# Attention block with feed-forward on one core: the stores of the maxima rows are issued by ScalarE instead of SyncE

## Chip, core and metric

One core of one Trainium2 chip. The metric is the device time of one execution in microseconds, as the median of several runs. TensorE (PE; PEld is its weight load), VectorE (DVE), ScalarE (ACT), GpSimd (POOL) and SyncE (SP) each run their own list of instructions and meet through semaphores. A DMA is issued by one of the engines and carried out by 16 DMA engines.

## What is computed

The inputs are x (32 batches of 100 tokens, 320 features) and a context (32 batches of 361 tokens, 192 features). There are 20 heads of 16 features, and everything is float32.

```python
h1 = _ln(x, n1_g, n1_b)
x = _attn(h1, h1, q1, k1, v1, o1_w, o1_b, heads) + x
h2 = _ln(x, n2_g, n2_b)
x = _attn(h2, context, q2, k2, v2, o2_w, o2_b, heads) + x
h3 = _ln(x, n3_g, n3_b)
proj = h3 @ ff_w1 + ff_b1
a, g = jnp.split(proj, 2, axis=-1)
ff = a * jax.nn.gelu(g, approximate=False) @ ff_w2 + ff_b2
return ff + x
```

_attn is softmax(q k / 4) v for each head, followed by the output projection.

## The kernel before

Three parts follow one another: a first stage (normalisation and q, k, v of the self attention for all batches, up to about 140 us), the attention loop, and the feed-forward. The change touches the second.

**The maximum rides in the product.** The softmax needs, for each query and head, its largest score. The scores are first formed with queries along the partitions (self_scores, cross_scores), and VectorE takes their negated maxima (maximum). The scores are then formed again with keys along the partitions (scores_for_exp), so that the exponentials can go straight into the product with v. So that the maximum is subtracted there, it is laid into the query operand as additional rows: the stack qs has 128 rows, and rows 0 and 64 hold the maxima's high part and low part against rows of ones in the key stack ks. The way of the maxima is: TensorE transposes them (turn_max, work jobs MT1 for self and MT2 for cross attention), ScalarE copies the high part into max_parts (max_high), VectorE forms the low part (max_low), and two DMAs store the parts into rows 0 and 64 of qs (place_max, which calls store_max). scores_for_exp(a, b, 0, 0), the first of attention a and batch b, waits for their landing on max_landed. Everything up to the DMAs is done in SBUF and PSUM.

**Software pipeline.** A period p handles four batches at once: x = p (exponentials, v products and output of the cross attention), s = p + 1 (its scores and maxima), c = p + 2 (exponentials and output of the self attention, keys and queries of the cross attention) and f = p + 3 (maxima of the self attention). There are 29 periods with a lead_in before and a run_out behind. Within a period each engine has its order of work written out by hand.

- TensorE: scores_for_exp(1, c, g) for the five groups g, between them self_scores(f) and project_kc(c, 0); times_v(1, c, 0 to 4); then scores_for_exp(2, x, g, jt), 15 of them, interleaved with cross_scores(s, 0 to 9), turn_max(1, f), project_kc, project_out(1, c), project_vc and others; turn_max(2, s) is the last. The two banks expin of the products for exponentials are used in turn, so the product number e waits for the exponential e - 2 (probs_made).
- ScalarE: exponential(1, c, 0 to 4), with kc_high(c, 0) behind the third; copy_product(1, c); exponential(2, x, ...), 15 of them, with max_high(1, f), kc_high(c, 1), heads_high(1, c) and kc_high(c, 2) between; then the copies of the period's end.
- VectorE: the maxima, one for each pair of heads of the cross attention, with the low parts, divisions and normalisations between them. cross_scores(s, i + 1) waits for maximum(2, s, i).
- SyncE: all DMA issues, in this order: load_x(f), place_max(1, f), load_context(f), load_qkv1 (load_own, nine DMAs), place_kc(c, 0), place_kc(c, 1), place_q2(c) (seven DMAs), place_max(2, s), store_x2(x), place_kc(c, 2). An issue that waits holds all behind it.

In lead_in SyncE issues place_max for (1, 1), (1, 2) and (2, 0), in run_out for (2, 30) and (2, 31). The function as it stands on SyncE:

```python
def place_max(a, b):
    ...
    sp.wait_ge(*emptied((f"MT{a}", b, 0)))
    if b > 1:
        last = EXP_AT[a, b - 2, G - 1, 0 if a == 1 else 2]
        sp.wait_ge(exp_full[last % 2], last // 2 + 1)
    store_max(sp, qs[a][u], max_parts[a], max_landed[a][u])
```

The first wait is for max_low (it frees the bank of the transpose), the second that the stack's last reader two batches ago is done.

Of the kernel before, what the change touches and what calls it, by code (L numbers as in the profile page):

```python
# [7 lines left out]
F32 = mybir.dt.float32  # L8
# [14 lines left out]
G, HG = 5, 4  # L23
# [81 lines left out]
OWN = 9  # L105


def store_max(sp, stack, parts, landed):
    for part in range(2):
        dst = stack[64 * part:64 * part + 1].rearrange("p a c n -> p (a c) n")  # L110
        sp.dma_start(dst.bitcast(F32), parts[:, part, :].bitcast(F32)).then_inc(landed, 16)


def own_products(pe, banks, queries, keys, i):
# [55 lines left out]
EXP_AT = {job: i for i, job in enumerate(EXP)}  # L170
# [107 lines left out]
def attention_phase(nc, held, early, x_in, ctxT, n1_g, n1_b, qkv1, o1_w, o1_b, n2_g, n2_b, q2_w, k2, v2, o2_w, o2_b,  # L278
# [8 lines left out]
    with ExitStack() as ctx:  # L287
# [19 lines left out]
        qs = {1: [at(f"qs1_{u}", [P, 2, HP, N], own[u]) for u in range(2)], 2: two("qs2_", [P, 2, HC, N], F32R)}  # L307
# [14 lines left out]
        max_landed = {1: sem2("max1_landed"), 2: sem2("max2_landed")}  # L322
# [61 lines left out]
        def emptied(job):  # L384

            k, n = WORK_AT[job]
            return work_empty[k], n + 1
# [10 lines left out]
        def _(sp):  # L398
# [62 lines left out]
            def place_max(a, b):  # L461
                if b is None:
                    return
                u = b % 2
# [5 lines that stand above are left out]
# [67 lines left out]

            def period(x, s, c, f, e):
                load_x(f)
                place_max(1, f)  # L540
                load_context(f)
                load_qkv1(e)
                place_kc(c, 0)
                place_kc(c, 1)
                place_q2(c)
                place_max(2, s)
                store_x2(x)
                place_kc(c, 2)

# [746 lines left out]
        def _(act):  # L1296
# [27 lines left out]
            def kc_high(b, t):  # L1324
                if b is None:
                    return
                job = ("KC", b, t)
                act.wait_ge(*filled(job))
                if b:
                    act.wait_ge(kc_landed[t][(b - 1) % 2], 16 * 3 * ((b - 1) // 2 + 1))  # L1330
                m = 32 * KT[t][1]
                nc.scalar.copy(kc_parts[0:m, 0, t, :], bank(job)[0:m, 0:JP]).then_inc(hi_made["KC"], 1)

            def max_high(a, b):
# [5 lines left out]
                    act.wait_ge(max_landed[a][(b - 1) % 2], 32 * ((b - 1) // 2 + 1))  # L1340
                nc.scalar.copy(max_parts[a][:, 0, :], bank(job)[0:ROWS[a], 0:N]).then_inc(hi_made[f"MT{a}"], 1)

            def copy_vc(b, i):
                if b is None:
                    return
                job, n = ("VC", b, i), JT[i][1]
                act.wait_ge(*filled(job))
                if b == 0 and i == 0:
                    act.wait_ge(ones_set, 1)
                if b > 1:  # L1350
                    act.wait_ge(pv_made, PV_AT[2, b - 2, G - 1] + 1)
                nc.scalar.copy(vc[b % 2][0:n, i, :, 0:DH], heads(bank(job)[0:n, 0:D]))\
                    .then_inc(work_empty[WORK_AT[job][0]], 1)

            def exponential(a, b, g, jt):
                if b is None:
                    return
                e = EXP_AT[a, b, g, jt]
                n = JT[jt][1] if a == 2 else N
                act.wait_ge(exp_full[e % 2], e // 2 + 1)  # L1360
                if e >= NPT:
                    act.wait_ge(pv_made, PV_AT[EXP[e - NPT][:3]] + 1)
                nc.scalar.activation(probs[e % NPT][0:n, :], expin[e % 2][0:n, 0:HG * N], ACT.Exp, scale=SCALE)\  # L1363
                    .then_inc(probs_made, 1)
# [58 lines left out]
            def run_out():  # L1423
                exponential(1, 31, 0, 0)
                exponential(1, 31, 1, 0)
                exponential(1, 31, 2, 0)
                exponential(1, 31, 3, 0)
                exponential(1, 31, 4, 0)
                kc_high(31, 0)
                copy_product(1, 31)  # L1430
                exponential(2, 29, 0, 0)
                exponential(2, 29, 0, 1)
                exponential(2, 29, 0, 2)
                heads_high(1, 31)
                exponential(2, 29, 1, 0)
                exponential(2, 29, 1, 1)
                exponential(2, 29, 1, 2)
                kc_high(31, 1)
                exponential(2, 29, 2, 0)
                exponential(2, 29, 2, 1)  # L1440
                exponential(2, 29, 2, 2)
                exponential(2, 29, 3, 0)
                features_high("T2", 31)
                exponential(2, 29, 3, 1)
                exponential(2, 29, 3, 2)
                copy_q2(31)
                exponential(2, 29, 4, 0)
                q2_high(31)
                exponential(2, 29, 4, 1)
                exponential(2, 29, 4, 2)  # L1450
                copy_product(2, 29)
                copy_vc(31, 0)
                max_high(2, 30)
                kc_high(31, 2)
                exponential(2, 30, 0, 0)
                copy_vc(31, 1)
                exponential(2, 30, 0, 1)
                exponential(2, 30, 0, 2)
                exponential(2, 30, 1, 0)
                exponential(2, 30, 1, 1)  # L1460
                exponential(2, 30, 1, 2)
                copy_vc(31, 2)
                exponential(2, 30, 2, 0)
                exponential(2, 30, 2, 1)
                exponential(2, 30, 2, 2)
                exponential(2, 30, 3, 0)
                heads_high(2, 29)
                exponential(2, 30, 3, 1)
                exponential(2, 30, 3, 2)
                exponential(2, 30, 4, 0)  # L1470
                exponential(2, 30, 4, 1)
                max_high(2, 31)
                exponential(2, 30, 4, 2)
                copy_product(2, 30)
                exponential(2, 31, 0, 0)
                exponential(2, 31, 0, 1)
                exponential(2, 31, 0, 2)
                exponential(2, 31, 1, 0)
                exponential(2, 31, 1, 1)
                exponential(2, 31, 1, 2)  # L1480
                exponential(2, 31, 2, 0)
                exponential(2, 31, 2, 1)
                exponential(2, 31, 2, 2)
                exponential(2, 31, 3, 0)
                exponential(2, 31, 3, 1)
                heads_high(2, 30)
                exponential(2, 31, 3, 2)
                exponential(2, 31, 4, 0)
                exponential(2, 31, 4, 1)
                exponential(2, 31, 4, 2)  # L1490
                tile_high(0)
                tile_high(1)
                copy_product(2, 31)
                heads_high(2, 31)
                tile_high(2)

            def period(x, s, c, f):
                exponential(1, c, 0, 0)
                exponential(1, c, 1, 0)
                exponential(1, c, 2, 0)  # L1500
                kc_high(c, 0)
                exponential(1, c, 3, 0)
                exponential(1, c, 4, 0)
                copy_product(1, c)
                exponential(2, x, 0, 0)
                exponential(2, x, 0, 1)
                max_high(1, f)
                exponential(2, x, 0, 2)
                exponential(2, x, 1, 0)
                exponential(2, x, 1, 1)  # L1510
                exponential(2, x, 1, 2)
                kc_high(c, 1)
                exponential(2, x, 2, 0)
                heads_high(1, c)
                exponential(2, x, 2, 1)
                kc_high(c, 2)
                exponential(2, x, 2, 2)
                exponential(2, x, 3, 0)
                exponential(2, x, 3, 1)
                exponential(2, x, 3, 2)  # L1520
                exponential(2, x, 4, 0)
                exponential(2, x, 4, 1)
                exponential(2, x, 4, 2)
                features_high("T2", c)
                copy_product(2, x)
                copy_vc(c, 0)
                copy_q2(c)
                copy_vc(c, 1)
                q2_high(c)
                heads_high(2, x)  # L1530
                copy_vc(c, 2)
                max_high(2, s)
# [1107 lines left out]
```

## Time and profile before

| | |
|---|---|
| median of 3 runs | 1357.21 us (1355.14 to 1361.05) |
| the profiled execution | 1353.17 us |
| its span, first to last instruction | 1351.3 us |
| granted TensorE clock, mean | 0.991 of full |
| TensorE busy | 1294.8 us |
| VectorE busy | 824.2 us |
| ScalarE busy | 681.8 us |
| GpSimd busy | 381.4 us |
| DMA issues of maxima rows | 128, all by SyncE |

The times of instructions come from the one profiled execution. Busy time counts work, not waiting, and not the issuing of DMAs.

### The profile page before, as it was taken

The numbers are of one execution on the slowest core, as the hardware profiler recorded it, in microseconds if no ns is written. First come the engines' busy times: TensorE is split into PE (matmuls) and PEld (weight loads), VectorE is DVE, ScalarE is ACT, GpSimd is POOL, SyncE is SP. The second block draws the span as 40 slices with busy tenths as digits, with TensorE's granted clock in tenths as the row PEclk, the third lists the DMA queues.
The fourth block names the chain that finished last, engine by engine and source line by source line (L and its number), as shares of the span: only waits on it lengthen the run. The fifth ranks groups of instructions, "written<-read, shape, count | busy, mean of one in ns | idle before, by whom it ended". The sixth has DMA issues, their size and how long they took to land. (4 is left out here: it accounts for less than half of the span.)

```text
span 1351.3 us, 35359 instructions
## 1 busy us (share of the span) xinstructions
PE 1294.8 (96%) x13364; PEld 1202.7 (89%) x13364; DVE 824.2 (61%) x1728; ACT 681.8 (50%) x1558; POOL 381.4 (28%) x545
## 2 busy tenths in 40 slices
PE   5999789999999999999999999999899999999999
PEld 4999678898898899889898898888689999999999
DVE  5555377777777777777777777777664324252521
ACT  4664345565565565565566566565554231313131
POOL 5421212212212212212212212222176243333331
PEclk8999799999999999999999999999999999999999
DMA  4677455445445455445544444443202101010000
GB/s 124 230 256 228 157 152 156 122 131 161 123 127 159 148 146 161 154 141 153 162 127 141 147 127 138 149 128 95 64 24 74 49 2 49 0 49 0 24 1 25
DMA packets 121669, 155.60 MB, mean 115 GB/s; under 512 B 25012, under 2 KB 115372, under 8 KB 121516
## 3 DMA queue, kind: packets, MB, share of 16 engines
q1 hardware_dynamic: 121516, 153.52, 37.3%
q8 instruction: 101, 1.65, 0.5%
q14 instruction: 52, 0.43, 0.1%
HBM read 62.98 MB, written 28.93 MB: 68 GB/s over the span
## 5 line engine op out<-in xcount | busy, mean ns | idle before, releaser
L1363 ACT ACTIVATE probs<-expin 120x400 f32<-120x400 f32 (+2 forms) x640 | 314.4, 505 | 165.5 <-PE expin L702 108.2
L1037 DVE TENSOR_REDUCE neg_max<-score 100x2 f32<-100x722 f32 x320 | 290.1, 907 | 62.1 <-PE score L676 49.4
L702 PE MATMUL expin<-qs,ks 128*120 128x200 f32 (+2 forms) x1280 | 236.1, 275 | 14.2 <-DMA qs<-max_parts 7.9
L702 PEld LDWEIGHTS expin<-qs,ks 128*120 128x120 f32 (+2 forms) x1280 | 191.9, 179 | 33.3 <-DMA qs<-max_parts 17.5
L676 PE MATMUL score<-ks,qs 128*100 128x362 f32 x640 | 165.5, 340 | 5.6 <-DVE neg_max L1037 4.2
L2427 DVE SCALAR_TENSOR_TENSOR hidden<-ps_a,b_cols,gelu 128x320 f32<-128x320 f32 x100 | 55.1, 551 | 165.1 <-PE ps_a L2351 165.1
L1550 POOL TENSOR_TENSOR var_eps<-mv,eps 100x1 f32<-100x1 f32 x32 | 6.1, 190 | 419.5 <-DVE mv L1105 419.5
L2589 POOL TENSOR_TENSOR hid_lo<-hidden,hid_hi 128x320 fp32r<-128x320 f32 x100 | 87.9, 879 | 122.4 <-ACT hid_hi L2497 122.2
L2509 ACT ACTIVATE gelu<-ps_g,b_cols 128x320 f32<-128x320 f32 x100 | 52.7, 527 | 136.9 <-PE ps_g L2351 136.9
L125 DVE TENSOR_REDUCE neg_max<-score 100x10 f32<-100x1000 f32 x62 | 74.4, 1200 | 54.2 <-PE score L118 54.2
L1570 POOL TENSOR_TENSOR ctx_hi<-ctx_raw,one 128x724 fp32r<-128x724 f32 x32 | 44.6, 1393 | 192.0 <-issue 177.6
L676 PEld LDWEIGHTS score<-ks,qs 128*100 128x100 f32 x640 | 83.0, 166 | 17.1 <-DVE neg_max L1037 6.5
L725 PE MATMUL attn<-probs,vc 120*17 120x100 f32 (+1 forms) x3840 | 96.5, 250 | 0.1
L2351 PE MATMUL ps_g<-t_hi,w_hi 128*128 128x320 f32 x300 | 92.2, 312 | 1.8 <-DVEq L2266 1.8
L725 PEld LDWEIGHTS attn<-probs,vc 120*17 120x17 f32 (+1 forms) x3840 | 80.2, 97 | 13.0 <-issue 7.8
L2351 PE MATMUL ps_a<-t_hi,w_lo 128*128 128x320 f32 x300 | 91.6, 311 | 0.0
L2351 PE MATMUL ps_a<-t_hi,w_hi 128*128 128x320 f32 x300 | 91.6, 310 | 0.0
L2351 PE MATMUL ps_g<-t_hi,w_lo 128*128 128x320 f32 x300 | 91.4, 310 | 0.0
L2368 PE MATMUL ps_y<-w_hi,hid_hi 128*128 128x320 f32 x250 | 78.5, 314 | 0.0
L2369 PE MATMUL ps_y<-w_lo,hid_hi 128*128 128x320 f32 x250 | 77.2, 309 | 0.0
L2370 PE MATMUL ps_y<-w_hi,hid_lo 128*128 128x320 f32 x250 | 77.1, 309 | 0.0
L1810 PE MATMUL qk_ps<-ks,w_qkv 128*128 128x400 f32 x320 | 68.8, 359 | 2.9 <-issue 2.9
(201 smaller groups left out, 2960.9 us busy)
## 6 DMA issues: line engine op xcount, KB each, us to landing
ks<-kc_parts SPq DMA_DIRECT2D x192, 181.0 KB, 3.0
qk_dram<-qk_parts SPq DMA_DIRECT2D x32, 500.0 KB, 5.2
qs<-q_parts SPq DMA_DIRECT2D x192, 75.0 KB
ks<-qk_dram SPq DMA_DIRECT2D x96, 125.0 KB
ctx_raw<-in_ctxT SPq DMA_DIRECT2D x64, 180.5 KB
ks<-kc_parts SPq DMA_DIRECT2D x96, 90.5 KB, 2.2
qs<-qk_dram SPq DMA_DIRECT2D x64, 125.0 KB
v_dram<-v_rows SPq DMA_DIRECT2D x32, 132.8 KB
```

The costliest lines, as they stand in the source:

```text
L125: return nc.vector.tensor_reduce(neg_max[:, :, n * i:n * (i + 1)], src, AX_X, ALU.max, negate=True)
L676: mm = pe.matmul(score[0:N, a, 0:JP], qs[2][u][:, a, q_slot(c), :], ks[2][u][:, c, :], start=True, stop=True)
L702: mm = pe.matmul(dst, ks[a][u][:, c, j0:j0 + n], qs[a][u][:, :, q_slot(c) if a == 2 else c, :], start=True, stop=True)
L725: mm = pe.matmul(attn[32 * i:32 * i + D1, g * N:(g + 1) * N], v, probs[EXP_AT[a, b, g, jt] % NPT][0:n, i * N:(i + 1) * N], start=(jt == 0) ...
L1037: ins = nc.vector.tensor_reduce(dst, src, AX_X, ALU.max, negate=True)
L1363: nc.scalar.activation(probs[e % NPT][0:n, :], expin[e % 2][0:n, 0:HG * N], ACT.Exp, scale=SCALE)\
L1810: mm = pe.matmul(qk_ps[m % 4][:, 0:W], w, a, start=(i == 0), stop=(i == 7))
L2351: mm = pe.matmul(bank[:, 0:W], a, b, start=(k == 0), stop=(k == len(passes) - 1))
L2368: pe.matmul(y, hid_hi[:, f, c], w2_hi[:, f, :], start=(f == 0), stop=False)
L2369: pe.matmul(y, hid_hi[:, f, c], w2_lo[:, f, :], start=False, stop=False)
L2370: mm = pe.matmul(y, hid_lo[:, f, c], w2_hi[:, f, :], start=False, stop=(f == FT - 1))
L2589: nc.gpsimd.tensor_tensor(hid_lo[:, f, c], hidden[n % 2][:], hid_hi[:, f, c].bitcast(F32), ALU.subtract).then_inc(hid_lo_made, 1)
```

## The change

Of the places in a period, place_max(1, f) and place_max(2, s) are taken out of SyncE's list. ScalarE gets a place_max of its own: for the cross attention of batch x in front of the third exponential of the next period (the batch that was s is then x), for the self attention of batch f behind exponential(2, x, 1, 2). Batch 29's is issued in run_out, and batch 0's stays in SyncE's lead_in, as do the others of lead_in and run_out. The semaphores and the data are the same.

```diff
-def store_max(sp, stack, parts, landed):
+def store_max(queue, stack, parts, landed):
     for part in range(2):
         dst = stack[64 * part:64 * part + 1].rearrange("p a c n -> p (a c) n")
-        sp.dma_start(dst.bitcast(F32), parts[:, part, :].bitcast(F32)).then_inc(landed, 16)
+        queue.dma_start(dst.bitcast(F32), parts[:, part, :].bitcast(F32)).then_inc(landed, 16)
...
             def period(x, s, c, f, e):
                 load_x(f)
-                place_max(1, f)
                 load_context(f)
                 load_qkv1(e)
                 place_kc(c, 0)
                 place_kc(c, 1)
                 place_q2(c)
-                place_max(2, s)
                 store_x2(x)
                 place_kc(c, 2)
...
+            def place_max(a, b):
+                act.wait_ge(*emptied((f"MT{a}", b, 0)))
+                if b > 1:
+                    last = EXP_AT[a, b - 2, G - 1, 0 if a == 1 else 2]
+                    act.wait_ge(exp_full[last % 2], last // 2 + 1)
+                store_max(act, qs[a][b % 2], max_parts[a], max_landed[a][b % 2])
+
...
             def run_out():
                 exponential(1, 31, 0, 0)
                 exponential(1, 31, 1, 0)
+                place_max(2, 29)
                 exponential(1, 31, 2, 0)
...
             def period(x, s, c, f):
                 exponential(1, c, 0, 0)
                 exponential(1, c, 1, 0)
+                if x:
+                    place_max(2, x)
                 exponential(1, c, 2, 0)
...
                 exponential(2, x, 1, 1)
                 exponential(2, x, 1, 2)
+                place_max(1, f)
                 kc_high(c, 1)
                 exponential(2, x, 2, 0)
```

## Rows read from the trace of the kernel before

**Rows 1.** The page's first part: busy time, share of the span, instructions.

```profile
PE 1294.8 (96%) x13364; PEld 1202.7 (89%) x13364; DVE 824.2 (61%) x1728; ACT 681.8 (50%) x1558; POOL 381.4 (28%) x545
```

**Rows 2.** 29 periods: busy PE, PEld, DVE, ACT, POOL; clock, DMA share, GB/s.

```profile
187.50:929.20 741.70, 728.39 (x9280) 663.50 (x9281) 554.84 (x1044) 448.92 (x1044) 163.58 (x174) 1.00 0.47 141
```

**Rows 3.** Who waited for whom, 190 to 950 us: total, times, longest.

```profile
PE expin L702 <- DMA qs<-max_parts: 7.9, 16, 1.1
...
PEld expin L702 <- ACT probs L1363: 1.1, 4, 0.6
```

**Rows 4.** Transposes of the maxima, all 29 periods, then one period alone.

```profile
L687 PE MATMUL work<-identf,neg_max x59: 245/247/253, 187.6 to 929.2; 100*24 100x100 f32 x30, 100*20 100x100 f32 x29
...
L687 PE MATMUL work<-identf,neg_max x3: 247/247/251, 776.1 to 801.3; 100*24 100x100 f32 x2, 100*20 100x100 f32 x1
```

**Rows 5.** Timeline of SyncE's issues: start, duration, line.

```profile
569.34 3.74 SPq L457 DMA_DIRECT2D qs<-q_parts  x6
573.19 1.66 SPq L111 DMA_DIRECT2D qs<-max_parts  x2
574.89 0.49 SPq L475 DMA_DIRECT2D x_dram<-x  x1
...
579.87 1.59 SPq L111 DMA_DIRECT2D qs<-max_parts  x2
```

**Rows 6.** Timeline of the other engines at the cross maxima, same period.

```profile
571.72 0.23 ACT L1341 CAST max_parts<-work 24x100 fp32r<-24x100 f32 x1 [1.34 <-PE work L687]
...
571.99 0.25 DVE L1056 TENSOR_TENSOR max_parts<-work,max_parts 24x100 fp32r<-24x100 f32 x1 [0.69 <-ACT max_parts L1341]
...
573.08 0.90 ACT L1363 ACTIVATE probs<-expin 100x400 f32<-100x400 f32 x2 [0.57 <-PE expin L702]
...
575.64 1.05 PE L725 MATMUL attn<-probs,vs 100*17 100x100 f32 x40
...
577.42 0.46 PE L702 MATMUL expin<-qs,ks 128*120 128x200 f32 x2 [0.72 <-DMA qs<-max_parts]
```

**Rows 7.** Timelines: store and use in a waiting period, then in one without.

```profile
266.99 1.65 SPq L111 DMA_DIRECT2D qs<-max_parts  x2
...
270.01 0.46 PE L702 MATMUL expin<-qs,ks 128*120 128x200 f32 x2 [0.49 <-DMA qs<-max_parts]
...
803.08 1.66 SPq L111 DMA_DIRECT2D qs<-max_parts  x2
...
806.55 0.46 PE L702 MATMUL expin<-qs,ks 128*120 128x200 f32 x2
```

**Rows 8.** SyncE's issues that write qs, whole span: duration min/median/max in ns.

```profile
L457 SPq DMA_DIRECT2D qs<-q_parts x192: 538/594/1802, 164.9 to 951.6; - x192
L111 SPq DMA_DIRECT2D qs<-max_parts x128: 727/787/1583, 136.7 to 971.3; - x128
```

**Rows 9.** ScalarE's queue: semaphore instructions before the third exponential and kc_high.

```profile
L1362 ACTq EVENT_SEMAPHORE  x1: 17/17/17, 573.1 to 573.1; - x1
...
L1330 ACTq EVENT_SEMAPHORE  x1: 17/17/17, 573.3 to 573.3; - x1
```

**Rows 10.** Timeline behind exponential (2, x, 1, 2), same period.

```profile
581.20 0.51 ACT L1363 ACTIVATE probs<-expin 121x400 f32<-121x400 f32 x1 [0.56 <-PE expin L702]
...
581.60 0.46 ACT L1332 CAST kc_parts<-work 128x362 fp32r<-128x362 f32 x1
...
581.94 0.53 ACT L1363 ACTIVATE probs<-expin 120x400 f32<-120x400 f32 x1
...
582.33 0.43 ACT L1302 CAST t_hi_OT<-work 128x300 fp32r<-128x300 f32 x1
...
583.24 0.70 PEld L593 LDWEIGHTS work<-w_o,t_hi_OT 128*100 128x100 f32 x5
...
583.33 0.91 DVE L1037 TENSOR_REDUCE neg_max<-score 100x2 f32<-100x722 f32 x1
...
584.60 0.26 PEld L676 LDWEIGHTS score<-ks,qs 128*100 128x100 f32 x2
```

## Prediction

> **What bounds the kernel now.** I read the page's head first: TensorE is busy for 96% of the span, ScalarE for 50% [rows 1]. That is an average over three parts; the change touches only the middle one, the 29 periods of the attention loop, so I cut that stretch out. From 187.5 to 929.2 us TensorE is busy 728.39 of 741.70 us at full clock, ScalarE 448.92 [rows 2]. So TensorE's own order of work sets the time, and a wait counts only where TensorE stands still. The table of waits names those places: the first products of a pair wait for the landing of the maxima rows (7.9 us on the matmuls), while its weight loads wait for ScalarE's exponentials 1.1 us [rows 3]. I then asked how long a period is. The transposes of the maxima stand once per half period, 59 of them from 187.6 to 929.2 us, so 29 periods take 741.6 us, 25.57 each [rows 4]. The period from 776.1 to 801.3 has no such wait and takes 25.23 us [rows 4]. The difference, 0.34 us, times 29 is 9.9 us: all that a better landing of the maxima can give, 0.7%.
>
> Where it comes from: SyncE issues the six stores of q2 back to back (3.74 us), and only then begins the two maxima stores at 573.19, though VectorE had finished the rows at 572.24 [rows 5, 6]. TensorE wants them at 577.42 and has stood 0.72 us [rows 6]. From issue to that use it takes 3.02 us in a usual waiting period (266.99 to 270.01) [rows 7]; in a period where the stores begin at 803.08 the use at 806.55 has no wait [rows 7]. There are slower ones, as at 573.19 (4.2 us). The maxima for the self attention (stored at 579.87, used a period half later) are waited for by nobody.
>
> **The change part by part.** Two stores in each of 58 places (29 for each attention) go from SyncE's queue to ScalarE's: 116 of 128 DMA issues; 12 stay. Nothing is added on another engine, and the data is the same.
>
> *What an issue costs.* No DMA is issued by ScalarE in this trace. The nearest rows are the same stores on SyncE: 727 ns at least, 787 median [rows 8], a pair 1.59 or 1.66 us [rows 5]. The cheapest store of any kind here is 0.49 us, the q2 stores 594 ns [rows 5, 8]. I take D = 1.6 us for a pair, with 1.0 (two at 0.49) and 2.8 (two at 0.8, each also waiting for one of SyncE's at 0.59) as ends. I take it that ScalarE runs nothing that stands behind an issue until it is over. When may it begin? The semaphore instructions between ScalarE's operations tell: the one in front of the third exponential runs at 573.1, when the wait of the second (started 573.08) has just been met, and the one in front of the copy of kc runs at 573.3, before the third exponential has started [rows 9]. So ScalarE's queue runs ahead of execution, but not past an instruction that still waits. The stores begin when the exponential before them starts.
>
> *Place A, cross maxima, after the second self exponential.* Start 573.1, as early as SyncE at its best (1.77 us after the transpose of the maxima at 801.31, here 1.66) and never held by the q2 stores. 3.02 us later is 576.1, TensorE needs them at 576.7 once its times-V products are over. Thus the 0.34 us go. In exchange the third exponential waits for the issues: 573.15 + D, then steps of 0.39 and 0.34 us (to a copy of kc and from it, as at 581.94 and 581.60 [rows 10]), 0.40 us to the fifth exponential and its 0.50 us (a pair takes 0.90 [rows 6]) end at 574.8 + D = 576.4. The last times-V group, of five in 1.05 us from 575.64, begins at 576.48 [rows 6]. So D = 1.6 just fits, about 0.05 us too much; every tenth more of D is a tenth more of period. Place A: -0.29 us.
>
> *Place B, self maxima, after exponential (2, x, 1, 2).* It starts at 581.20, and the copy of kc at 581.60, an exponential at 581.94 and the copy of the turned heads at 582.33, ending 582.76, follow without a gap [rows 10]. With the issues the first starts at 581.25 + 1.59 + 0.05 = 582.89, 1.29 us late, and the turned heads are ready at 584.05. TensorE loads its weights for project_out at 583.24, 0.48 us after the heads before; now, with 0.05 us for the signal (an estimate: the copy that ends at 571.95 frees VectorE at 571.99 [rows 6]), it stalls 0.86 us (the products into the expin bank that the delayed exponential frees stall 0.7 of it). VectorE's low part of the heads comes behind that copy, then its maximum of 0.91 us, on which the next cross_scores waits: 584.12 + 0.47 + 0.91 = 585.50 against TensorE's 584.60 + 0.86 = 585.46 [rows 10]; about 0.1 us more. Place B: +0.95 us, or D - 0.65. Nothing later absorbs it: the free period has hardly an idle TensorE, and all chains of the second half start from project_out.
>
> *What SyncE gains.* store_x2 and the last kc stores begin up to 1.7 us earlier, and load_context and the nine loads of load_own are no longer behind the wait of place_max(1, f). The loop's table of waits [rows 3] has no entry of TensorE for their tiles, so 0. Were they late, the next self_scores would pay. But they now run while ScalarE issues, in both places: SyncE's stores and own loads follow one another there for microseconds, as its six q2 stores do [rows 5].
>
> The Trainium skill, page "DMA: Bandwidth & Descriptors", section "Issuing engines are not separate DMA queues", says that issuing from several engines saves only the time of the sequencer, usually small beside the transfer. By the rows it is 1.66 us of 3.02, over half [rows 5, 7]; were it small, place B would cost nothing and the change would give its 9.9 us or less.
>
> *Sum.* 29 x (-0.29 + 0.95) = 29 x 0.66 = 19.1 us. The profiled execution took 1353.17 us (span 1351.3), 4 us under the median of 1357.21; 1372.3 on its scale is 1376.3 on that of the median. The break-even is at D = 0.99: (D - 0.65) - 0.34 = 0.
>
> **The rivals.**
> *R1, one descriptor generator.* If ScalarE's issue must wait while SyncE's is being served, each store takes up to 0.59 us more [rows 8]. D = 2.8: place B 2.15, place A -0.34 + 1.2 = 0.86, together 3.0 us, 87 us, 1444 us. If only half of an issue excludes the other, D = 2.2: 1.55 + 0.26 = 1.8 us, 52 us, 1410 us. For it: both engines issue at once in A and B. Against: no row shows it, all packets are SyncE's. The Trainium skill has this rule: "Perfetto Trace Analysis", section "DMA Instruction — HWDGE (DVE, Sync)", has a lock on the descriptor generator, shared by two sequencers. No run here shows it yet.
> *R2, the other side: ScalarE issues cheaply.* At D of 0.65 or less place B costs nothing and the whole 9.9 us come in: 1347 us; at D = 0.99 no change. For it: 0.49 us for the x2 store. Against: the same stores have no case under 0.727 us in 128.
> *R3, the landing isn't earlier.* The change does not do what it is for: the small stores, now beside SyncE's kc stores instead of behind q2, still land late, as at 573.19. Then A gives nothing: 29 x (0.95 + 0.05) = 29 us, 1386 us. For it: waits of over 0.7 us occur also where SyncE began at its earliest. Against: 3.02 us repeats.
>
> **How the numbers follow.** Forecast, D between 1.5 and 1.75 a pair: chance 0.48, 1376 us, its own range 1369 to 1386. R3 0.08. R1 0.21, half of it above 1410. R2 0.16 for a gain over 0.5% (6.8 us, what a measurement of this kernel can tell from no change), and 0.07 for between. So faster 0.16, same 0.07, slower 0.77. The range goes from 1347, R2's full gain, to 1412, R1's half price; some 0.12 lies outside.
>
> **What the profile after would show.** 116 issues on ScalarE of about 0.8 us each (R1: 1.1 or more, R2: under 0.5). The third exponential of a period 1.6 us behind the second. The wait for the landing gone from TensorE's table, and new ones there, for the exponential's expin bank and for the turned heads, together about 0.9 us a period, near place B. Periods of 26.2 us with TensorE's clock unchanged. Wrong I would be if ScalarE went on with arithmetic during an issue, if the issue began before the exponential in front had its input, or if TensorE found the lost 0.9 us again in the second half.

## The result and the profile after

The changed kernel takes 1384.68 us (median of 6 runs, 1381.05 to 1386.62) against 1356.18 us for the kernel before in the same rounds: a ratio of 1.0199, 95% interval 1.0178 to 1.0220. It is slower by 28.5 us; the forecast was 19.1 us slower, at 1376. The profiled execution has a span of 1382.8 us, 31.5 more than before.

The page's first part after the change, to be held against [rows 1]: the same instructions, TensorE 22 us busier, and a span that grew more. Of the 22 us, 14.7 lie in the loop. Part of them is the way in which a product behind a stall is recorded, with 0.46 us instead of 0.36 at place B; the rest wasn't followed up. The second fence is the page's part on DMA queues; queue 10 is new.

```profile
PE 1316.7 (95%) x13364; PEld 1207.6 (87%) x13364; DVE 828.8 (60%) x1728; ACT 677.6 (49%) x1558; POOL 382.0 (28%) x545
...
q10 hardware_dynamic: 3828, 1.03, 0.3%
```

The length of the loop comes first, as in [rows 4], from the row of the same transposes after the change.

```profile
L685 PE MATMUL work<-identf,neg_max x59: 246/247/253, 188.8 to 957.1; 100*24 100x100 f32 x30, 100*20 100x100 f32 x29
```

29 periods take 768.3 us instead of 741.6: 26.7 us of the 31.5 lie in the loop. What TensorE waits for there is in the table of waits after, 190 to 965 us; it answers to [rows 3].

```profile
ACT kc_parts L1330 <- issue: 33.2, 28, 1.7
DVE kc_parts L1054 <- ACT kc_parts L1330: 30.8, 30, 3.2
...
PEld expin L700 <- ACT probs L1368: 25.2, 32, 1.4
...
PE expin L700 <- ACT probs L1368: 15.2, 29, 1.1
...
PE expin L700 <- DMA qs<-max_parts: 4.7, 6, 1.2
```

The wait for the landing went from 16 times and 7.9 us to 6 times and 4.7 us. In its place stands a wait of TensorE for an exponential, 29 times in 29 periods. The first line shows whose doing it is: ScalarE stands 1.2 us before its copy of kc, in 28 periods, with no input missing ("issue").

The stores themselves, from the rows of the tile qs, against [rows 8]:

```profile
L111 ACTq DMA_DIRECT2D qs<-max_parts x116: 724/742/1332, 197.7 to 958.7; - x116
...
L111 SPq DMA_DIRECT2D qs<-max_parts x12: 751/803/1279, 136.1 to 1000.7; - x12
```

An issue by ScalarE takes 742 ns in the median, 45 ns less than one by SyncE before, and as long at its shortest.

**Place B, self maxima.** Timelines of ScalarE, VectorE and TensorE after the change in one period; the operations are those of [rows 10], 12.08 us earlier on the clock.

```profile
569.12 0.50 ACT L1368 ACTIVATE probs<-expin 121x400 f32<-121x400 f32 x1 [0.55 <-PE expin L700]
569.18 1.50 ACTq L111 DMA_DIRECT2D qs<-max_parts  x2
570.78 0.46 ACT L1330 CAST kc_parts<-work 128x362 fp32r<-128x362 f32 x1 [1.16 <-issue]
571.13 0.51 ACT L1368 ACTIVATE probs<-expin 120x400 f32<-120x400 f32 x1
571.53 0.42 ACT L1300 CAST t_hi_OT<-work 128x300 fp32r<-128x300 f32 x1
...
571.98 0.47 DVE L1049 TENSOR_TENSOR t_lo_OT<-work,t_hi_OT 128x300 fp32r<-128x300 f32 x1 [0.17 <-ACT t_hi_OT L1300]
572.37 0.90 DVE L1035 TENSOR_REDUCE neg_max<-score 100x2 f32<-100x722 f32 x1
...
571.69 0.29 PEld L700 LDWEIGHTS expin<-qs,ks 128*121 128x121 f32 x2 [0.80 <-ACT probs L1368]
571.70 0.46 PE L700 MATMUL expin<-qs,ks 128*121 128x200 f32 x2 [0.48 <-ACT probs L1368]
572.09 0.95 PE L591 MATMUL work<-w_o,t_hi_OT 128*100 128x320 f32 x5
```

The issues begin 0.06 us after the start of the exponential in front of them, last 1.50 us, and the copy of kc follows 0.10 us behind their end: 1.66 us after the exponential instead of 0.40, so 1.26 us late (forecast 1.29). The product into the bank that the delayed exponential frees stalls, its weight load by 0.80 us, and project_out runs behind it, 2.97 us after the exponential's start. Before it was 583.33 - 581.20 = 2.13, from this row of TensorE:

```profile
583.33 0.90 PE L593 MATMUL work<-w_o,t_hi_OT 128*100 128x320 f32 x5
```

That is 0.84 us lost. The turned heads were ready at 571.95, and TensorE has no wait for them in the table: by the profile the wait that ended last was the one for the bank.

**Place A, cross maxima.** The same for the third self exponential, against [rows 6].

```profile
561.66 0.50 ACT L1368 ACTIVATE probs<-expin 100x400 f32<-100x400 f32 x1 [0.57 <-PE expin L700]
561.72 1.51 ACTq L111 DMA_DIRECT2D qs<-max_parts  x2
563.33 0.50 ACT L1368 ACTIVATE probs<-expin 100x400 f32<-100x400 f32 x1 [1.17 <-PE expin L700]
...
564.07 0.91 ACT L1368 ACTIVATE probs<-expin 100x400 f32<-100x400 f32 x2
...
564.27 1.13 PE L723 MATMUL attn<-probs,vs 100*17 100x100 f32 x40
565.33 0.46 PE L700 MATMUL expin<-qs,ks 128*120 128x200 f32 x2
```

Here the stores land in time: 3.61 us from their beginning to the use, which has no wait. The times-V products are stretched, 1.13 us for 1.05, as the last group meets the delayed fifth exponential: that one ends at 564.98 and the group begins at 565.04. (The row calls the third exponential's wait "PE expin", but those products were done by 561.81; what it waited for was the issue.) In another period the landing is late although it began as early, at 428.37:

```profile
432.99 0.46 PE L700 MATMUL expin<-qs,ks 128*120 128x200 f32 x2 [0.93 <-DMA qs<-max_parts]
```

### The profile page after: what moved, and what is told of

Read it like the earlier page. It is cut to its first block and busy times, and to the rows that moved or that the text cites. A ratio compares the mean times of both kernels' runs of the same rounds, so it can differ in the third digit from the quotient of the medians.

```text
span 1382.8 us, 35359 instructions
## 1 busy us (share of the span) xinstructions
PE 1316.7 (95%) x13364; PEld 1207.6 (87%) x13364; DVE 828.8 (60%) x1728; ACT 677.6 (49%) x1558; POOL 382.0 (28%) x545
## 5 line engine op out<-in xcount | busy, mean ns | idle before, releaser
L700 PE MATMUL expin<-qs,ks 128*120 128x200 f32 (+2 forms) x1280 | 241.1, 279 | 26.5 <-ACT probs L1368 16.4
```

Of the source, the lines that this page charges most:

```text
L700: mm = pe.matmul(dst, ks[a][u][:, c, j0:j0 + n], qs[a][u][:, :, q_slot(c) if a == 2 else c, :], start=True, stop=True)
```

## Experiments

The period splits at the two transposes of maxima. The first half (cross transpose to self transpose, mostly 6.3 to 7.5 us) holds place A, the second (19 us) place B. The two columns of halves are means over the 29 periods, from the starts of the transposes in the timeline; "landing" is TensorE's matmul row for the landing of maxima in the table of waits, 190 to 950 us (965 for the change). Each ratio is to the kernel before in the same rounds. Its median there was 1356.18 beside the change, 1356.36 beside cross_only, self_only, self_late and self_half, 1354.30 beside sync_early and cross_earlier, and 1356.80 beside clear_early.

| kernel | median us | ratio to before (95%) | first half | second half | landing |
|---|---|---|---|---|---|
| before | 1356.18 | | 6.68 | 18.89 | 7.9 |
| the change | 1384.68 | 1.0199 (1.0178 to 1.0220) | 6.69 | 19.80 | 4.7 |
| cross_only | 1355.45 | 0.9985 (0.9966 to 1.0005) | 6.75 | 18.94 | 6.5 |
| self_only | 1383.17 | 1.0198 (1.0162 to 1.0233) | 6.62 | 19.81 | 6.2 |
| self_late | 1353.98 | 0.9981 (0.9959 to 1.0003) | 6.64 | 18.88 | 3.7 |
| self_half | 1358.44 | 1.0019 (1.0000 to 1.0039) | 6.65 | 19.07 | 7.6 |
| sync_early | 1362.74 | 1.0063 (1.0042 to 1.0084) | 6.86 | 18.95 | 2.7 |
| cross_earlier | 1357.36 | 1.0020 (1.0004 to 1.0037) | 6.71 | 18.88 | 2.6 |
| clear_early | 1347.61 | 0.9933 (0.9914 to 0.9952) | 6.38 | 18.90 | 0.2 |

**cross_only and self_only: one place each.** cross_only puts the self attention's stores back on SyncE, self_only the cross attention's.

```diff
 # cross_only, from the changed kernel
                 load_x(f)
+                place_max(1, f)                # SyncE
                 load_context(f)
...
                 exponential(2, x, 1, 2)
-                place_max(1, f)                # ScalarE
```

```diff
 # self_only, from the changed kernel
                 place_q2(c)
+                place_max(2, s)                # SyncE
                 store_x2(x)
...
                 exponential(1, c, 1, 0)
-                if x:
-                    place_max(2, x)            # ScalarE, and the one in run_out
```

> Only the cross attention's stores are issued by ScalarE; the self attention's stay with SyncE. Theory 1 (the cost is the delay of the ScalarE operations behind the stores at the self attention's place; at the cross attention's place the saved landing wait and a new delay cancel): the half period from the cross transpose to the self transpose keeps its mean of about 6.7 us, the other half is back at 18.88, the time is 1356 to 1359. Theory 2 (every issue by ScalarE costs the same, wherever it stands): half of the 28.5 us, 1370.

> Only the self attention's stores are issued by ScalarE. Theory 1: half periods of 19.77 instead of 18.88 us, 29 x 0.9 = 26 us, so 1382. Theory 2: 1370.

The whole loss is in self_only (27 us, second half 19.81); cross_only can't be told from before. Both have 58 issues by ScalarE, so the cost isn't one of issuing as such. TensorE's wait for an exponential follows the place too. This is its row in the table of waits, first of self_only, then of cross_only:

```profile
PE expin L701 <- ACT probs L1369: 15.2, 29, 1.1
...
PE expin L701 <- ACT probs L1369: 0.7, 2, 0.4
```

**self_late: the same 116 issues, one place moved.**

```diff
                 exponential(2, x, 1, 2)
-                place_max(1, f)
                 kc_high(c, 1)
...
                 exponential(2, x, 3, 1)
+                place_max(1, f)
                 exponential(2, x, 3, 2)
```

> All 116 stores stay with ScalarE, but the self attention's are moved seven exponentials later, in front of exponential (2, x, 3, 2), where ScalarE stood idle for 1.75 us waiting for TensorE. Theory 1: the issues lie in that gap, the second half period is back at 18.9 us, the time is 1356 to 1360. Theory 2 (each issue costs), or theory 3 (SyncE's loads, now earlier, are what costs): nothing changes, 1385.

The loss is gone, 1353.98 us. ScalarE's timeline shows the two issues in a gap that was there anyway (the exponential behind waits 1.75 us for TensorE's attn products, as long as before). SyncE's loads come early here too: load_context begins 0.6 us before the self transpose in the median period, in the change 1.0 us before it, in the kernel before 2.9 us behind it. So the earlier loads aren't the cause either.

```profile
585.57 1.04 ACT L1368 ACTIVATE probs<-expin 120x400 f32<-120x400 f32 x2 [0.65 <-PE expin L700]
586.16 1.52 ACTq L111 DMA_DIRECT2D qs<-max_parts  x2
588.36 0.90 ACT L1368 ACTIVATE probs<-expin 121x400 f32<-121x400 f32 x2 [1.75 <-PE attn L723]
```

**self_half: half the issue time at place B.** From self_only; ScalarE stores the high row, SyncE the low row at its old place.

```diff
                 exponential(2, x, 1, 2)
-                place_max(1, f)
+                place_max(1, f, which=(0,))    # ScalarE: high parts
                 kc_high(c, 1)
...
                 load_x(f)
+                place_max(1, f, which=(1,))    # SyncE: low parts
                 load_context(f)
```

> At the self attention's place ScalarE issues only the store of the high parts (0.75 us); SyncE issues that of the low parts and both cross stores, as before. Theory 1, a margin of about 0.45 us before TensorE stands: the copy of kc starts 0.5 us late, TensorE stands at most 0.1 us a period, 0 to 3 us in all, so 1356 to 1360. Theory 2, proportional to the issues: half of 26, 1369.

ScalarE's timeline, one period:

```profile
586.05 0.51 ACT L1370 ACTIVATE probs<-expin 121x400 f32<-121x400 f32 x1 [0.56 <-PE expin L702]
586.11 0.73 ACTq L111 DMA_DIRECT2D qs<-max_parts  x1
586.94 0.46 ACT L1332 CAST kc_parts<-work 128x362 fp32r<-128x362 f32 x1 [0.38 <-issue]
```

The copy of kc comes 0.89 us after the exponential instead of 0.40, and half the issue time leaves a seventh to a fifth of the cost: the second half is 19.07 us (median 19.01 against 18.88), the time 1358.44, 0.19% over before, which is just clear of no change. The loss isn't proportional to the issues. There is a margin: 0.49 us of delay cost 0.13 to 0.18 us, 1.26 us cost 0.91, so it is 0.3 to 0.4 us (expected was 0.45).

**sync_early: the landing without ScalarE.** All stores on SyncE, the cross maxima's in front of the last two q2 stores.

```diff
                 for slot, part in ((0, 0), (2, 0), (1, 1)):
                     if part:
+                        place_max(2, s)
                         sp.wait_ge(*emptied(("QT", b, 0)))
```

> All stores stay with SyncE as in the kernel before, but the two cross stores are issued in front of the last two of the six q2 stores, so they begin as soon as VectorE has made the rows (about 0.85 us after the transpose instead of 1.75 to 2.97). Theory 1 (the landing wait is SyncE's queue, and a landing delayed by an instruction fetch needs about 1.2 us more): the wait for the landing goes, first half periods of 6.35 throughout, 29 x 0.33 = 9.6 us less, 1347. Rival (the landing is late through other transfers, whenever it is begun): no change, 1356.

This missed: 0.63% slower. The maxima do go out early, 0.8 to 1.4 us after the transpose in all but the first period, and the landing waits fall to 2.7 us, 2.3 of them in that first period. But the two q2 stores behind them are late now. They are used directly after the maxima: cross_scores of the next batch waits for q2_landed one product later. The timelines of SyncE and TensorE:

```profile
578.01 1.66 SPq L111 DMA_DIRECT2D qs<-max_parts  x2
579.72 1.24 SPq L458 DMA_DIRECT2D qs<-q_parts  x2
...
582.40 0.46 PE L702 MATMUL expin<-qs,ks 128*120 128x200 f32 x2
583.54 0.55 PE L676 MATMUL score<-ks,qs 128*100 128x362 f32 x2 [0.68 <-issue]
```

The profile names no releaser for the 0.68 us ("issue"); that it is q2_landed is read from the code. In the table of waits, 190 to 950 us, the line stands 12 times with 7.7 us, once behind the loop with 1.5. My expectation had looked at who waits for the maxima and not at who waits for what they were put in front of.

**cross_earlier: place A one exponential earlier.** From self_late.

```diff
                 exponential(1, c, 0, 0)
-                exponential(1, c, 1, 0)
                 if x:
                     place_max(2, x)
+                exponential(1, c, 1, 0)
                 exponential(1, c, 2, 0)
```

> All 116 stores by ScalarE, the self ones late as in self_late, the cross ones one exponential earlier, in front of the second self exponential. Theory 1: they begin at 0.85 instead of 1.70 us after the transpose and land in time in every period, also beside an instruction fetch; but the second exponential starts at 2.45 instead of 1.64, and the product that uses its bank again stalls 0.35 us. First half periods 6.7 us, all alike, 1354 to 1358. Rival: landings are as late as before in some periods, and the stall comes on top, 1365.

The landing waits go, but for 2.6 us, 2.5 of them in the first period. The first half has a floor (its usual shortest value) of 6.56 us instead of self_late's 6.46: the stall at the exponentials eats what the landing gives. 1357.36 us against 1354.30, no gain.

**clear_early: the queue shortened where it was idle.** All stores on SyncE in the old order; clear_max, which writes rows 0 and 64 and needs no q2, goes in front of the wait for q2.

```diff
             def place_q2(b):
...
-                sp.wait_ge(hi_made["Q2"], b + 1)
                 cross_stack_free(b, G - 1)
                 clear_max(sp, qs[2][u], zeros, q2_landed[u])
+                sp.wait_ge(hi_made["Q2"], b + 1)
```

> Everything stays with SyncE; only the clearing store of a period's q2 (clear_max) is issued in front of the wait for the q2 rows, in which SyncE stood idle, instead of behind it. So the six q2 stores and the two cross stores all begin 0.6 us earlier; the cross stores begin 1.1 us after the transpose instead of 1.75 or more, and no q2 store is put behind them. Theory 1 (TensorE waits at the first cross product for whatever is last in SyncE's queue): the landing waits of 8 us go but for the slowest landings, 1347 to 1351. Rival (the landing time is set by other transfers): 1355.

1347.61 us, 0.67% faster than the kernel before and the best of all. The cross stores begin 1.1 to 2.2 us after the transpose, mostly 1.1 to 1.3, where it was 1.75 to 2.97. SyncE's and TensorE's timelines, one period, and the table of waits:

```profile
587.86 0.58 SPq L84 DMA_DIRECT2D qs<-zeros  x1
588.94 4.62 SPq L457 DMA_DIRECT2D qs<-q_parts  x6
593.66 1.67 SPq L111 DMA_DIRECT2D qs<-max_parts  x2
...
596.90 0.46 PE L702 MATMUL expin<-qs,ks 128*120 128x200 f32 x2
```

```profile
PE expin L702 <- DMA qs<-max_parts: 0.2, 1, 0.2
```

Its loop takes 733.1 us, 8.5 less than before, of the 9.9 us that [rows 4] allowed.

## Why the prediction was right, and where it was off

**The bound and the size of the prize** were right. TensorE's order sets the period, and its waits for the landing cost 9.9 us at most; clear_early collects 8.5 of them, while the second half stays as it was (18.90).

**What an issue costs**: D was taken as 1.6 us a pair from SyncE's rows and measures 1.50 or 1.51 in the rows above. That the stores begin with the exponential in front of them, and that nothing behind them runs before they are over, is in all timelines above (0.06 us after its start, 0.10 us to the next operation).

**Place B**: forecast +0.95 us a period, measured 19.80 - 18.89 = 0.91. The delays came as written: copy of kc 1.26 us, turned heads 1.28 us, project_out 0.84 us (forecast 1.29, 1.29 and 0.86). In one point the profile differs: it puts TensorE's stall down to the expin bank (0.80 us, forecast were 0.7 of the 0.86) and shows no wait for the turned heads, which the list of signs had also named. self_late shows that the place makes the cost, self_half the margin.

**Place A is the step that failed**: "Thus the 0.34 us go." Forecast was -0.29 us a period, measured is 0.01 (6.69 against 6.68), and cross_only alone gives nothing that can be measured. 8.4 us of gain were in the sum and none came; with the 1 us too much at place B that is the difference between 19.1 us and the loop's 26.7.

Two sizes were wrong. The price of delaying the fifth exponential is 0.11 us, not 0.05: the first half's floor went from 6.35 to 6.46, though D came out smaller than assumed. And 3.02 us from store to use is only one of two cases. In six of 29 periods after the change it was 4.0 to 4.9 us, and these waits (4.7 us) don't go by beginning at 1.70 instead of 1.77 us after the transpose. Together that is 6.4 of the 8.7 us missing at place A; the rest lies in waits too short for the table and wasn't followed up.

The trace of before had this in it. Of its 16 waiting periods, 8 have the 3.0 us, all with stores held up by the q2 stores. In 7 others SyncE began 1.75 to 1.87 us after the transpose, as early as it could, and the use still came 3.75 to 4.66 us later: 4.1 of the 7.9 us, out of reach for this change. The 8 did go (3.6 us), and the floor's 0.11 us in each of 29 periods (3.2 us) took that back. I had seen a 4.2 us case and left it in R3 at a chance of 0.08, where it belonged in the sum. cross_earlier and clear_early, which mostly begin 0.6 us earlier or more, do absorb nearly all: 0.2 us of landing waits are left in each, cross_earlier's first period aside.

So the total came out right with one of its two terms wrong. 1384.68 lies at the upper end of the forecast's own range, nearer to R3's 1386 than to 1376; that it is inside is owed to the width of the range and not to place A.

**The rivals.** R1, one issue excluding the other, is out at the price that I gave it: all 116 of ScalarE's issues run beside one of SyncE's, and they take 742 ns in the median, no more than SyncE's own. The rule of the Trainium skill, "Perfetto Trace Analysis", section "DMA Instruction — HWDGE (DVE, Sync)", that the sequencers which share the descriptor generator lock it for one another, has no visible cost for ScalarE here. Some of SyncE's issues grew: clearing stores took up to 2257 ns after 989, nine of them over 0.9 us where it had been one, with the median at 576 after 585. An issue of ScalarE beside them isn't needed for that: in self_late ten of them took 1.1 to 2.3 us, and none of these had an issue of ScalarE beside it. What it is stays open; TensorE's table of waits has no entry for these stores or for the loads behind them. R2 is out: no issue was under 0.72 us. R3 came true in its result, place A giving nothing, though its late landings were six periods and not all. SyncE's gain was 0, as costed. The other 4.8 us of the profiled span, 1.2 before the loop and 3.6 behind it, I haven't explained; by the medians the whole loss is 28.5, which leaves some 2 us outside the loop.

## What to carry to other kernels

Moving a DMA issue to ScalarE moved its whole issue time (0.75 us here) into ScalarE's order, though ScalarE was busy for only half of the span. If an issue has to go to such an engine, put it directly in front of an operation that waits for another engine longer than that, as in self_late. If a landing is late because its queue is busy, look first for something in that queue that can be issued in an idle stretch ahead of it, and before reordering ask who waits for each store that gets later. Cost a landing by its slow cases, not by the usual one.

## What was not expected of the hardware

In 8 of the 16 waiting periods before, the first product could use the rows 3.0 us after the beginning of the two stores (9.4 KB each), but in 13 cases with a wait in the table (7 before, 6 after) it came only 3.7 to 4.9 us after it. In each of the 13 a packet of the instruction queue (q8, 16 KB, 0.9 to 1.8 us) began between 0.3 us before and 2.4 us after the store's beginning. The DMA view of the changed kernel from 852 to 857 us, around the slowest, has it in its list of queues:

```profile
q1 hardware_dynamic: 467, 0.52, 37.5%
q10 hardware_dynamic: 72, 0.02, 1.8%
q8 instruction: 1, 0.02, 1.8%
```

The other traces point the same way. Over before, the change, cross_only, self_only, self_late and self_half, a q8 packet began 1.1 to 2.5 us after the store in 58 of 174 periods, and 35 of these were late (use 3.7 us or more after the store, with a wait of over 0.1 us); of the other 116 periods 2 were. The bounds were set after looking, 23 stores beside such a packet landed in time too, and no run here changed the instruction fetches. So this is a strong coincidence and not a shown cause.
